# Moving an odd batch's transposes into the pass ahead, and other edits to the queue orders of a Perceiver kernel

## The reference, cut to what matters

```python
# x (32, 64, 128): latents; ctx_1024 (32, 1601, 128); mask: which context rows count
x = x + xattn(ctx_1024, layernorm(x), mask, ...)   # 16 heads of 64
x = x + attn(layernorm(x), ...)                    # 16 heads of 8, with slopes
x = x + ffn(layernorm(x), ...)                     # 8-bit fake quantisation
# xattn: k, v from concat(layernorm(ctx), layernorm(latents)); q from the latents;
#        softmax over the masked keys; out @ Wout; layernorm
```

## Time and profile before

| | us |
|---|---|
| median of 3 runs (lowest, highest) | 866.89 (865.94, 867.53) |
| the profiled execution | 870.95 |
| its span, first to last instruction | 869.2 |
| TensorE busy in the span | 780.4 (90%) |
| VectorE, ScalarE, GpSimd busy | 605.6, 587.0, 521.7 |

### The profile page before, as it was taken

The page is one execution under the profiler, slowest core; times in us unless marked ns, Lnnn a source line. Parts: engine busy times, 40 slices in busy tenths (PEclk is TensorE's granted clock), DMA queues, the critical chain, the costliest instruction groups (busy, mean ns, idle before and its releaser), DMA issues.

```text
span 869.2 us, 22523 instructions
## 1 busy us (share of the span) xinstructions
PE 780.4 (90%) x7063; PEld 423.7 (49%) x7063; DVE 605.6 (70%) x1515; ACT 587.0 (68%) x1017; POOL 521.7 (60%) x660
## 2 busy tenths in 40 slices
PE   5697899999999999999999999999999999997753
PEld 4343444545455455545454545545554545454412
DVE  5787566676777776666767677767666776756487
ACT  5387577776767676868777676767676877763242
POOL 3277356676757666666767675766666676764101
PEclk9799899999999999999999999999999999999655
DMA  6212212121221112121212122110212121200001
GB/s 191 56 42 81 71 43 68 43 62 52 57 56 52 49 26 63 41 72 38 71 41 61 52 57 56 54 48 26 62 41 72 39 71 40 67 17 16 4 0 49
DMA packets 98349, 45.86 MB, mean 53 GB/s; under 512 B 65956, under 2 KB 90376, under 8 KB 98184
## 3 DMA queue, kind: packets, MB, share of 16 engines
q1 hardware_dynamic: 98256, 45.37, 18.8%
q10 hardware_dynamic: 56, 0.05, 0.0%
HBM read 25.70 MB, written 3.27 MB: 33 GB/s over the span
## 4 chain that ended last, share of the span: by engine, by line
PE 65%; DVE 19%; ACT 7%; issue 7%; POOL 1%; DVEq 1%; DMA 1%; ACTq 1%; SPq 0%; POOLq 0%
PE bank L1399 14%; PE bank L1458 7%; DVE mx L1799 7%; PE bank L1362 7%; PE bank L1317 5%; PE bank L1366 5%; PE bank L1364 4%; PE bank L1475 3%; PE bank L1519 3%; PE bank L1334 3%; PE bank L1504 2%; PE bank L1494 2%; ACT arena L1080 2%; ACT arena L1065 2%; DVE xtT_l L1782 1%
## 5 line engine op out<-in xcount | busy, mean ns | idle before, releaser
L832 POOL TENSOR_TENSOR p<-arena,p 128x512 f16<-128x512 f32 x256 | 299.5, 1170 | 180.3 <-ACT arena L1065 179.5
L1062 ACT ACTIVATE p<-bank,maskbias 128x512 f16<-128x512 f32 x224 | 155.2, 693 | 138.2 <-PE bank L1366 137.6
L1799 DVE TENSOR_REDUCE mx<-bank 128x1 f32<-128x512 f32 x256 | 165.8, 685 | 37.9 <-PE bank L1334 36.6
L1399 PE MATMUL bank<-p,xv 128*128 128x512 f16 (+1 forms) x768 | 183.9, 382 | 5.2 <-ACT arena L1080 2.7
L1065 ACT ACTIVATE arena<-bank,maskbias 128x512 f32<-128x512 f32 x224 | 154.3, 689 | 0.0
L1399 PEld LDWEIGHTS bank<-p,xv 128*128 128x128 f16 (+1 forms) x768 | 58.0, 97 | 73.2 <-issue 23.1
L1795 DVE TENSOR_TENSOR qkl_l<-bank,qkl_h 128x512 f16<-128x512 f32 x64 | 41.1, 686 | 71.1 <-ACT qkl_h L1048 71.1
L1362 PE MATMUL bank<-qkc_h,xtT_h 128*128 128x512 f16 (+1 forms) x256 | 87.1, 390 | 0.0
L1334 PE MATMUL bank<-xtT_h,qkc_h 128*128 128x448 f16 x256 | 86.5, 359 | 0.0
L1366 PE MATMUL bank<-qkc_h,xtT_l 128*128 128x512 f16 (+1 forms) x256 | 85.4, 381 | 0.0
L1364 PE MATMUL bank<-qkc_l,xtT_h 128*128 128x512 f16 (+1 forms) x256 | 85.2, 380 | 0.0
(11 more groups left out here) (266 smaller groups left out, 1532.3 us busy)
## 6 DMA issues: line engine op xcount, KB each, us to landing
arena<-den_dram SPq DMA_DIRECT2D x62, 128.0 KB, 3.2
qkc_h<-arena SPq DMA_DIRECT2D x30, 256.0 KB, 2.4
qkc_l<-arena SPq DMA_DIRECT2D x30, 256.0 KB, 2.4
raw<-in_ctx SPq DMA_DIRECT2D x32, 192.0 KB, 2.5
raw<-in_ctx SPq DMA_DIRECT2D x64, 32.0 KB, 2.2
lt<-lt_dram SPq DMA_DIRECT2D x60, 32.0 KB, 2.1
arena<-in_L_xattn_Wkv SPq DMA_DIRECT2D x1, 1024.0 KB, 7.1
ltT_dram<-x_all SPq DMA_DIRECT2D x4, 256.0 KB, 2.9
```

The costliest lines, as they stand in the source:

```text
L832: g.tensor_tensor(p_halves[0:r, slot, 1, :], p_all[0:r, (plan.halves_made(0, k, t) - 1) % 2, :], p_halves[0:r, slot, 0, :], ALU.subtract). ...
L1062: a.activation(p_halves[0:r, slot, 0, :], sbank[t % SRING][0:r, :], ACT.Exp, bias=bias)
L1399: op = mm(bk[:, :], halves_of[at, row, :], p_halves[at, slot, prob, :], start=tile < 2 and n == 0, stop=last and n == 2)
L1799: v.tensor_reduce(mx[:, hq_tile, part:part + 1], bk[:, 0:width], AX.X, ALU.max).then_inc(s_jobs_taken, 1)
```

## The change

- T of the odd batch goes to half step 15.5 of the pass ahead (`AHEAD`, a job of k = 3). Pass 0 has a job table of its own (`FIRST_BODY`), with its T at step 0 and the new one at 15.5; the last pass has none. On VectorE its eviction stands between `tail` and the XF operations, which are now a function of their own (`final`).
- SyncE: `load_queries(plan, i + 2)` stands behind the second load of context of pass i. Block 1 is stored in pass 0, block 2 in the first half and block 3 in the second half of pass 1, each behind the load of latents. The transposed latents in DRAM have room for a pair 16 (written from the last one), which the last load reads and nothing uses.
- ScalarE: the copies of the latents' accumulators stand between the two exponentials of their step.
- VectorE: CX stands ahead of the jobs of its whole step (`self_context`). RDEN of the odd batch goes from step 5 to 7.
- Passes 0 and 1: the steps of the latents' blocks and of ALIBI are others, moments 1 before pass 0's first step; waits for `lt` follow.

```diff
@@ -48,10 +48,11 @@
-LATE = dict(wv=[0, 1, 2, 4], lt=[None, 6, 10, 17], aw=[7])
-BLOCK_AT = {1: (1, 4, 7), 2: (7, 8, 11), 3: (9, 14, 17)}
-HALVES_AT = {1: (6, 7), 2: (9, 10), 3: (15, 16)}
-ALIBI_AT = 18
+LATE = dict(wv=[0, 1, 2, 4], lt=[None, 9, 17, 25], aw=[7])
+BLOCK_AT = {1: (-1, 8, 11), 2: (1, 15, 18), 3: (9, 24, 27)}
+ROOT_AT = {1: 1, 2: 3, 3: 11}
+HALVES_AT = {1: (9, 11), 2: (17, 19), 3: (25, 27)}
+ALIBI_AT = 16
 FFN = dict(scales=2, round=[3, 4], fw=[4, 5], fwd=[6], wd=[7])
...
@@ -93,9 +94,13 @@
         self.START = self.numbered(self.of_batch(0, at["START"]) + self.of_queries(at["START"]))
-        self.BODY = self.numbered(self.of_batch(1, at["ODD"]) + self.of_queries(at["NEXT"]) + self.of_batch(0, at["EVEN"]))
-        self.LAST = self.numbered(self.of_batch(1, at["ODD"]))
-        self.IN_START, self.IN_BODY = (sum(j.banks for j in jobs) for jobs in (self.START, self.BODY))
+        odd, inner = self.of_batch(1, at["ODD"]), self.of_queries(at["NEXT"]) + self.of_batch(0, at["EVEN"])
+        self.AHEAD = "AHEAD" in at
+        later = [j for j in odd if j[0] != "T"] if self.AHEAD else odd
+        if self.AHEAD:
+            inner += [("T", 3, m, at["AHEAD"][m], 1) for m in range(self.GROUPS)]
+        self.FIRST_BODY, self.BODY, self.LAST = self.numbered(odd + inner), self.numbered(later + inner), self.numbered(later)
+        self.IN_START, self.IN_FIRST, self.IN_BODY = (sum(j.banks for j in jobs) for jobs in (self.START, self.FIRST_BODY, self.BODY))
         assert self.IN_BODY % 2 == 0
...
@@ -118,16 +123,22 @@
-        return 0 if i is None else self.IN_START + i * self.IN_BODY
+        return 0 if i is None else self.IN_START + (0 if isinstance(i, int) and i == 0 else self.IN_FIRST - self.IN_BODY + i * self.IN_BODY)
-        return self.START if i is None else self.LAST if last else self.BODY
+        return self.START if i is None else self.LAST if last else self.FIRST_BODY if isinstance(i, int) and i == 0 else self.BODY
         return self.base(i) + job.first + job.banks
+
+    def transposed_through(self, i, last, par):
+
+        if par == 1 and self.AHEAD and not (isinstance(i, int) and i == 0):
+            return self.through(i - 1, False, "T", 3, self.GROUPS - 1)
+        return self.through(i, last, "T", par, self.GROUPS - 1)
...
@@ -170,10 +181,10 @@
     START=dict(QP=[-3, -3], QC=[-2, -2], QL=[-1, -1], T=[-2.5], MAX=[1, 1, 2, 2, 3, 3, 4, 4], MT=5),
-    ODD=dict(T=[0], MAX=[2.5, 3, 3, 3.5, 4, 4, 4.5, 5], MT=6),
+    ODD=dict(T=[0], MAX=[2.5, 3, 3, 3.5, 4, 4, 4.5, 5], MT=6), AHEAD=[15.5],
     NEXT=dict(QP=[0, 0.5], QC=[1.5, 6.5], QL=[8.5, 9.5]),
     EVEN=dict(T=[7.5], MAX=[10.5, 11, 11, 11.5, 12, 12, 12.5, 13], MT=14), XV={2: (0, 4)},
-    RDEN=(3, 5), MOVE=11, ST1=[3, 4, 5, 6], YN=[6, 7], XB=8, ST2=8, M0=9, P0=9, X1=10, X1B=17, M1=10, P1=11,
+    RDEN=(3, 7), MOVE=11, ST1=[3, 4, 5, 6], YN=[6, 7], XB=8, ST2=8, M0=9, P0=9, X1=10, X1B=17, M1=10, P1=11,
     XH=12, XHT=13, XHT_OUT=13, QKV=14, QKV_OUT=14, VBLK=15, KEXP=16, SC=17, ALIBI=[18, 20], SMAX=22, SHIFT=23, EXP=24,
...
@@ -663,6 +674,8 @@
                 sp.dma_start(ltT_dram[:, :, 512 * j:512 * j + 512].rearrange("s d q -> d s q"), ltT_all[:, j, :, :]).then_inc(s_lat_stored, 16)
+                if j == 3:
+                    sp.dma_start(ltT_dram[:, :, TOK:TOK + 2 * M].rearrange("s d q -> d s q"), ltT_all[:, j, :, 512 - 2 * M:512]).then_inc(s_lat_stored, 16)
...
@@ -711,8 +724,6 @@
                         more = not (last and k == 1)
-                        if k == 0 and since and not last:
-                            load_queries(plan, i + 1)
                         if since and k == 0:
...
@@ -721,6 +732,8 @@
                             load_ctx(plan, b + 2, par)
+                        if k == 1 and not last:
+                            load_queries(plan, i + 2)
                         if since or k == 1:
...
@@ -729,6 +742,9 @@
                             load_latents(b + 2, par)
+                        if k == 1 and since < 2:
+                            for j in ((1,), (3,))[since] if plan is WINDOW else ((1, 2, 3), ())[since]:
+                                store_block(j)
                         if since and k == 0:
...
@@ -737,17 +753,14 @@
                             rden_rows(b - 1, 1 - par, pair)
-                        if not since and k == 1:
-                            store_block(1)
+                        if since == 1 and k == 0 and plan is WINDOW:
                             store_block(2)
-                        if since == 1 and k == 0:
-                            store_block(3)
                         if k == 0:
                 body(1, 1, False)
-                sp.wait_ge(s_lat_stored, 128)
+                sp.wait_ge(s_lat_stored, 144)
                 with sp.Fori(2, PAIRS - 1) as i:
...
@@ -1047,22 +1060,25 @@
-            def probs(plan, i, k, t):
+            def probs(plan, i, k, t, part):
                 b = i * 2 + k
                 gg, tile, r, slot = b * plan.STEPS + t, plan.steps[t][0], plan.rows(t), slot_of(plan, k, t)
+                bias = zrow[0:r, :] if tile == 0 else maskbias[0:r, k, plan.chunk(tile):plan.chunk(tile) + 1]
+                if part == 1:
+                    if (k, t) in plan.SPLIT:
+                        made = plan.halves_made(i, k, t)
+                        if happened(made - 2):
+                            act.wait_ge(s_p_lo, made - 2)
+                        a.activation(p_all[0:r, (plan.halves_made(0, k, t) - 1) % 2, :], sbank[t % SRING][0:r, :], ACT.Exp, bias=bias).then_inc(s_probs_ready, 1)
+                    return
                 act.wait_ge(s_scores_ready, gg + 1)
                     act.wait_ge(s_maskbias_ready, b + 1)
-                bias = zrow[0:r, :] if tile == 0 else maskbias[0:r, k, plan.chunk(tile):plan.chunk(tile) + 1]
                 if (k, t) in plan.SPLIT:
-                    made = plan.halves_made(i, k, t)
                     a.activation(p_halves[0:r, slot, 0, :], sbank[t % SRING][0:r, :], ACT.Exp, bias=bias)
-                    if happened(made - 2):
-                        act.wait_ge(s_p_lo, made - 2)
-                    a.activation(p_all[0:r, (plan.halves_made(0, k, t) - 1) % 2, :], sbank[t % SRING][0:r, :], ACT.Exp, bias=bias).then_inc(s_probs_ready, 1)
                 else:
...
@@ -1141,14 +1157,15 @@
                         b = i * 2 + k
-                        probs(plan, i, k, t)
+                        probs(plan, i, k, t, 0)
+                        for h in range(2):
+                            if t == LAG + min(h, plan.LAT - 1):
+                                copy_latents_part(plan, b, i, k, h)
+                        probs(plan, i, k, t, 1)
                         background(plan, i, since, s, self_exp)
                             copy_context_part(plan, b - 1, i - 1 + k, 1 - k, t - LAG + 2)
-                        for h in range(2):
-                            if t == LAG + min(h, plan.LAT - 1):
-                                copy_latents_part(plan, b, i, k, h)
                         if s == plan.at["MOVE"]:
...
@@ -1232,12 +1249,14 @@
-            def late_weights(s):
+            def late_weights(s, since):
                         pe.wait_ge(*late_done(*LATE_JOBS[n - 2]))
+                    if (kind, k) == ("lt", 3) and since:
+                        pe.wait_ge(s_yn_done, 2)
                     if kind == "wv":
...
@@ -1444,7 +1463,7 @@
                         if not happened(p):
-                            pe.wait_ge(*late_done("lt", 3))
+                            pe.wait_ge(*late_done("lt", 2))
                         if happened(p) and not plan.own:
...
@@ -1826,6 +1846,21 @@
                 return v.tensor_scalar(dst, src, smv[:, r, 0:1], srs[:, r:r + 1], ALU.subtract, ALU.mult)
+
+            def self_context(plan, p, s):
+                at, two = plan.at, tail_banks(plan)[1]
+                if s == at["CX"]:
+                    dve.wait_ge(s_attn_b, p * 7 + 5)
+                    src = two[:, 0:8 * 18].rearrange("p (a b e) -> p a b e", b=2, e=AE + 1)
+                    v.reciprocal(sden[:, :, :].unsqueeze(3), src[:, :, :, AE:AE + 1]).then_inc(s_sden_ready, 1)
+                    dve.wait_ge(s_sden_ready, p + 1)
+                    v.tensor_tensor(cx[:, :].rearrange("p (a b e) -> p a b e", b=2, e=AE), src[:, :, :, 0:AE],
+                                    sden[:, :, :].unsqueeze(3).to_broadcast([P, 8, 2, AE]), ALU.mult).then_inc(s_cx_ready, 1)
+
+            def drained(plan, p, s):
+                self_context(plan, p, s)
+                tail(plan, p, s)
+                final(plan, p, s)
...
@@ -1928,13 +1958,19 @@
                         more = not (last and k == 1)
+                        if not since and s == 0:
+                            late_weights(-1)
                         prep(plan, i, last, s - 0.5)
+                        background(plan, i, since, s, self_context)
                         prep(plan, i, last, s)
```

(28 more changed lines are left out.)

14 lines of the change are left out of this document (4 added, 10 removed).

## The result

The kernel after takes 857.14 us (median, 856.92 to 857.94) against 867.21 us before; the ratio is 0.9884, 95% interval 0.9866 to 0.9903. It is faster by 1.2%, 10.1 us in place of the 23 that were forecast, and 857.14 lies just outside the forecast's range of 834 to 856. The profiled execution took 857.94 us, its span is 856.2 us.

The account below looks back on a forecast made before the run. TensorE was taken to set a pass's time, so its idle time could be won: 12.0 + 10.5 + 1.6 = 24.1 us off 870.95, less 4.06 for the median, 842.8; stated as 844, range 834 to 856.

Parts of the forecast that it names:

- Part 1: Odd batch's transposes T moved to the pass ahead: path to QP1 0.66 us shorter, 0.15 us counted a pass.
- rival B: Start of pass: xf beside GpSimd's 1.90 us operation makes QC0 0.45 us later; 0.3 gained a pass, 851 us; chance 0.20.
- Part 2: Latents' accumulator copies moved between two exponentials: values no longer wait, 0.28 us in the even half of a pass.
- Part 3: CX ahead of two even-batch maxima, reciprocals RDEN later: maxima and row maximum's transpose come 0.49 us earlier each pass.
- VectorE is without a gap in between: Even maxima: VectorE runs without idling up to the row maximum's transpose, so that transpose moves up by 0.49 us.
- rival E: Gaps close but the time returns at the next one, VectorE and TensorE handing two banks across: 865 to 868; chance 0.03.
- Steady passes: Thirteen like passes gain 0.15 + 0.28 + 0.49 = 0.92 us each, 12.0 us in all; bounds 0.3 to 1.4 a pass.
- Part 4: Passes 0 and 1: query load ahead of block stores, later block steps; both passes gain 10.5 us, bounds 5 and 14.
- Last pass: Pass 15: no transposes T (0.85 us), copies and CX moved as in the other passes (0.77): 1.6 us gained.
- the drain behind it keeps its order: 0: Work after the last pass stays in the same order, so nothing is gained or lost there.

Follow-up runs that it names:

- minus1: Kernel after with the odd batch's transposes put back at step 0 of the pass: 882.71 us, ratio 1.0172 to the kernel before.
- stats_split: Kernel after with two of the four statistics of the next batch's rows taken one step earlier: 859.60 us, ratio 0.9877 to the kernel before.
- act_split: Kernel after with xf made by ScalarE and two of four statistics one step earlier: 843.21 us, ratio 0.9698 to the kernel before.
- kexp_first: Kernel after with GpSimd's KEXP ahead of the difference at step 0 of a pass: 858.17 us, ratio 0.9887 to the kernel before.

## Why the prediction was wrong, by its own steps

**Part 1** is one of the two steps that failed. By the last values as the common point, the kernel after stands 11.51 us ahead. The prediction put the end of xf and its maximum at 422.35; it came at 422.52 (411.01), so the hold by the 1.90 us operation was costed well. It let QP0's eviction follow at once; in the trace 0.34 us lie between, and the chain of waits names them as VectorE's loop:

```profile
410.82 0.06 DVEq L1981
410.88 0.24 issue
```

Line 1981 is the loop over the pairs; before, this turn lay behind xf too, but T's eviction came first and waited for ScalarE anyway. So QC0 is at 424.28 in place of the prediction's 423.86 (424.06 with the 0.15 that its sum took): 0.07 us lost where 0.15 was counted, 0.22 a pass, 2.9 in all. That is rival B's mechanism, which had a chance of 0.20 (a pass gains 0.3 in it; measured 0.36), though B had QC0 0.45 late and not 0.07. That the path has at least 0.66 in it and that VectorE holds it down was right: with xf gone from VectorE QC0 comes 0.85 earlier than before. What no term held is how steep the hold is: minus1 and stats_split lose 1 to 3 us by a shift of some tenths.

**Part 2**: 0.28 forecast, 0.31 measured by taking it back.

**Part 3** is the other: 0.49 forecast, 0.13 by the trace, 0.08 by taking it back. The step "VectorE is without a gap in between" was true of before and was no longer true once CX had left the queue: 0.37 us became waits for TensorE's matmuls of the maxima. That is rival E at one place. In act_split, with two statistics in those waits, the 0.49 came out. 0.36 to 0.41 us a pass, 4.7 to 5.3 in all: the largest miss.

**Steady passes** so gave 0.36 us each, 4.7 in place of 12.0. This is a round sum: of the twelve from T to T in the traces the first gained 0.02 and the others 0.36, which makes the 4.0 above.

**Part 4 and passes 0 and 1**: 10.5 forecast, 9.9 in the trace; pass 1 runs at clock 1.00. But the sum was made against the profiled execution and 4.06 us then taken off as if every kernel had them. The part of them that is slow clock and waits in passes 0 and 1 was itself among the gains counted. In the medians part 4 is 7.0, 3.2 less than in the traces. That these 3.2 lie in passes 0 and 1 is argued, not shown: no execution of before near its median was profiled.

**Last pass**: 1.6 forecast. T's 0.85 us came to nothing, since without the jobs of a next pair the values of step 1 wait for KEXP, ahead of whose end they may not start (the wait stands in front of them):

```profile
735.50 1.90 POOL L905 TENSOR_TENSOR arena<-kT,halfmask 128x1024 f32<-128x1024 f32 x1
...
737.45 0.82 PE L1418 MATMUL bank<-p,xv 128*128 128x512 f16 x3 [0.87 <-POOL arena L905]
```

Then the tail took 2.2 us more, where the forecast had "the drain behind it keeps its order: 0". It goes with the second window at the lower level, which the trace of before doesn't have; the cause of that level stays open.

From 24.1 to 10.1 that is: 7.3 us missing in the steady passes, 0.6 in passes 0 and 1, 3.2 in the last pass and the tail, and 2.9 between the difference of the traces (13.0) and that of the medians.

## What to carry to other kernels

A copy, scale or two-input operation of VectorE on SBUF that started beside a long one of GpSimd lasted here until that one ended, so before such a queue is shifted, by as little as 0.2 us, look at what each will start beside, and give to another engine those on which a chain hangs. When an operation is taken out of a chain between two engines, its time is gained only up to the next wait for the other engine; put other work into that wait. Sum a forecast against an execution that is like the median, since gains read from the slow stretches of one that isn't may be only partly there in the rest (here 7.0 of 10.2 us).

## What the runs showed of the hardware that I had not expected

A VectorE operation that waits gets in between two GpSimd operations that follow one another without a gap, but only one of them: in kexp_first the copy ended 0.09 behind KEXP and xf, next in the queue, was held for the whole following difference. An operation whose second input is one column spread over the row (`to_broadcast`) was held like the others: 2.00 us. And the mean granted clock of one and the same kernel moved between 0.951 and 0.962 from run to run, worth some 5 us of 870.
